# First attention: value product turned round (probabilities moving, values standing), result folded back by a product, and three of four second halves made on Pool

## The chip, the cores and the metric

One core of a Trainium2 chip runs the whole program. The time is the device time of one launch in microseconds: a median of 1862.45 over three runs (1860.44 to 1863.14). The engines of the core work in parallel, each through its own queue in order, and wait for one another on semaphores: TensorE (PE), VectorE (DVE), ScalarE (ACT), GpSimd (Pool), and SyncE (SP), which here issues most DMAs.

## What is computed

Two layers over x (2 x 512 tokens, 512 wide), each an attention over a context (2 x 1024 rows) and a feed-forward part; the second layer has 8-bit quantised keys, values, probabilities and ternary weights. The change is in the first layer's attention alone. It is plain causal attention with 16 heads of 32, the queries being the normalised x, and keys and values being the context itself:

```
qh, kh, vh = heads of q, k, v
scores = einsum('bhqd,bhkd->bhqk', qh, kh) / sqrt(32)
causal = ki <= qi + (Sk - Sq)            # Sq 512, Sk 1024
attn = softmax(where(causal, scores, -10000))
out = einsum('bhqk,bhkd->bhqd', attn, vh)
```

What follows depends on it exactly enough that a router's choice must not flip, so the kernel keeps fp32 accuracy by splitting: keys, queries and values are each three bf16 parts that sum to the fp32 value, and the probabilities are two fp16 halves, p1 (the rounded value) and p2 (the rest).

## The kernel before

The stages follow each other: context and key/value projection for the second layer (to about 175 us), layer norm and splitting (to 213), the first attention (213 to 572), router and expert feed-forward (to about 1190), then the second layer.

The first attention has 32 units, one for each batch and head (`UNITS`), which `sweep` runs on each engine: two written out, fifteen turns of a loop of two, the rest written out. In a unit the 512 queries meet 1024 keys in 8 key tiles of 128 (`KT`); because of the mask tiles 4 to 7 need only 512, 384, 256 and 128 queries (`WID`), 3328 columns in all. They are handled in four groups of two tiles: 1024, 1024, 896 and 384 columns. What is done per unit, with the lines:

- PE turns keys (L709) and queries (L717, L719) with transposes, so that the head's parts lie on partitions. These go through one PSUM bank, bank6. ACT copies the keys out of it to kA (`copy_keys`, L1137), DVE copies the first 64 rows again to kC (L1410) and copies the queries (L1414, L1415).
- For the softmax's maximum PE makes rough scores of the *next* unit, query tile by query tile, in two halves of `scores` (`smax`, L732 to L735); DVE takes the maxima (`take_max`, L1420) and splits them in two bf16 parts (`split_m`, L1427, L1429); PE turns these (`turn_m`, L741) and ACT copies them to two rows of qC (`copy_m`, L1141), where the exact score product takes the maximum off by itself.
- Exact scores, transposed (keys on partitions), are made tile by tile in bank4 and bank5 (`st`, L756 to L759). ACT turns each into exp in fp32 (eP, L1150), and a group into p1 (fp16, L1155). DVE makes p2 = eP - p1 (`rest_of_p`, L1434).
- `pv` (L773): for each key tile and each query tile of 128 that the mask leaves, p1 and p2 stand in the array (128x128, fp16) and 97 columns of values move through it (three parts of 32 and a column of ones, whose result is the softmax's sum). These are 26 pairs, 52 products of 97 columns per unit; they collect in bank7 with queries on partitions.
- `finish_unit` on DVE: the three parts are summed (L1440), the sum's reciprocal taken (L1442) and the product written to oatt (L1444).

The order is written out by hand in each engine's `att_unit`. PE's: the next unit's maxima tiles 0 and 1, scores 2 and 3, maxima tile 2, scores 4 and 5, pv 0 and 1, maxima tile 3, scores 6 and 7, turn the keys of the unit after the next, pv 2 and 3, turn the maxima, turn the queries, scores 0 and 1 of the next unit, pv 4 to 7. The first product of those scores 0 and 1 needs the maxima's rows from ACT; its start (L756) serves below as the unit's mark, the "restart". ACT's: for each group two exp and p1, at the end the keys' copy and the maxima's copy. DVE's: finish the unit before, then maxima, subtractions and copies in turn. SP loads three pieces per unit (`stage_unit`, L442, L443, L446). Pool has no work between 215.6 us and the scatter at 615 us (L568).

Of the kernel before, what the change touches and what calls it, by code (L numbers as in the profile page):

```python
# [25 lines left out]
F32 = mybir.dt.float32  # L26
# [29 lines left out]
KROW = KBLK * HD + 2  # L56
QROW = QBLK * HD
K3 = 3 * HD
K2 = 2 * HD
# [5 lines left out]
CONSTS = 13  # L65
# [53 lines left out]
def program(nc, x, ctx_in, gate_w, w1, w2, w3, Wq, bq, Wkv, bkv, Wp, bp, w_gate, w_up, w_down, ln_w, out):  # L119
    with ExitStack() as stack:  # L120
# [11 lines left out]
        class Region:  # L132
# [28 lines left out]
        xres = keep.take(F32, NT, D)  # L161
        vint = keep.take(BF16, NC, D)
# [6 lines left out]
        ones = keep.take(BF16, P)  # L169
        iota_e = keep.take(F32, E)  # L170
# [26 lines left out]
        v_step, vmax_ready, v_stored, v_back, v_made = (  # L197
            sem(n) for n in ("v_step", "vmax_ready", "v_stored", "v_back", "v_made"))
# [36 lines left out]
        p2 = ra.take(F16, NP)  # L235
        mx = ra.take(F32, QT)
        mparts = ra.take(BF16, QT, 2)
        osum = ra.take(F32, QT, HD)
# [110 lines left out]
        st_done, exp_done, p1_done, p2_done = (sem(n) for n in ("st_done", "exp_done", "p1_done", "p2_done"))  # L349
        pv_done, oread_done, o_done = (sem(n) for n in ("pv_done", "oread_done", "o_done"))  # L350
# [3 lines left out]
        zero_made = sem("zero_made")  # L354
# [30 lines left out]
        wpiece_done, wsum_done, wsum_all, w_mean = (sem(n) for n in ("wpiece_done", "wsum_done", "wsum_all", "w_mean"))  # L385
# [16 lines left out]
        def _(sp):  # L402
# [26 lines left out]
            sp.wait_ge(zero_made, 1)  # L429
# [84 lines left out]
        def _(pool):  # L514
# [22 lines left out]
            made(pool.iota(iota_s, pattern=[[1, SLOTS + 1]], base=0, channel_multiplier=0, allow_small_or_imprecise_dtypes=True))  # L537
            assert n == CONSTS
            pool.memset(zero, 0.0).then_inc(zero_made, 1)
            pool.memset(kvrow[:, :, :, :, KBLK * HD:KROW].rearrange("p b h t c -> p (b h t) c"), 1.0).then_inc(ones_set, 1)  # L540

# [9 lines left out]
            pool.partition_all_reduce(svrow, vam, P, bass.bass_isa.ReduceOp.absmax).then_inc(vmax_ready, 1)  # L551
            pool.wait_ge(vmax_ready, 1)

            pool.wait_ge(wsum_done, 1)
            pool.partition_all_reduce(wst[:, 1], wst[:, 0], P, bass.bass_isa.ReduceOp.add).then_inc(wsum_all, 1)
            pool.wait_ge(wsum_all, 1)
# [3 lines left out]
            for a in range(2):  # L560
                pool.memset(kC[a][K2:K2 + 2, :], 1.0).then_inc(ones_set, 1)

# [89 lines left out]
        def _(pe):  # L652
# [109 lines left out]
            def pv(u, a, k, r, first):  # L762
                if k == 0:
                    pe.wait_ge(v_in[a], 16 * (r + 1))
                    if not first:
                        pe.wait_ge(oread_done, 2 * u)
                if k % 2 == 0:
                    pe.wait_ge(p2_done, 4 * u + k // 2 + 1)
                    pe.wait_ge(p1_done, 4 * u + k // 2 + 1)
                for t in range(max(0, k - HALF), QT):  # L770
                    c = OFF[k] + (t * P - (SQ - WID[k]))
                    for part in (p1, p2):
                        ins = pe.matmul(bank7[:, t * 97:t * 97 + 97], part[:, c:c + P], vst[a][:, k, HD:HD + 97],  # L773
                                        start=(k == 0 and t == 0 and part is p1), stop=(k == KT - 1 and t == QT - 1 and part is p2),
                                        skip_group_check=True)
                if k % 2:
                    ins.then_inc(pv_done, 1)

            def att_unit(u, a, r, first, last):
# [3 lines left out]
                st(u, a, 2, first); st(u, a, 3, first)  # L783
                if not last:
                    smax(u + 1, b, 2)
                st(u, a, 4, first); st(u, a, 5, first)
                pv(u, a, 0, r, first); pv(u, a, 1, r, first)
                if not last:
                    smax(u + 1, b, 3)
                st(u, a, 6, first); st(u, a, 7, first)  # L790
# [9 lines left out]
                pv(u, a, 4, r, first); pv(u, a, 5, r, first)  # L800
                pv(u, a, 6, r, first); pv(u, a, 7, r, first)
# [17 lines left out]
            pe.wait_ge(oread_done, 2 * UNITS)  # L819
# [244 lines left out]
        def _(act):  # L1064
# [60 lines left out]
            act.wait_ge(vmax_ready, 1)  # L1125
# [9 lines left out]
            def copy_keys(u, b):  # L1135
                act.wait_ge(k0_turned, at(u))
                act.activation(kA[b], bank6[:].bitcast(BF16), ACT.Copy).then_inc(ka_ready, 1)  # L1137

            def copy_m(u, b):
                act.wait_ge(m_turned, at(u))  # L1140
                act.activation(qC[b][K2:K2 + 2, :], scores[:, 0:512].bitcast(BF16)[K2:K2 + 2, 0:SQ], ACT.Copy).then_inc(m_ready, 1)  # L1141

            def att_unit(u, a, k, first, last):
                b = 1 - a
                for g in range(4):
                    for j in (2 * g, 2 * g + 1):
                        if j == 2 * g and not first:
                            act.wait_ge(p2_done, 4 * (u - 1) + g + 1)
# [7 lines left out]
                if within(u + 2, UNITS):  # L1156
                    copy_keys(u + 2, a)
                if not last:
                    copy_m(u + 1, b)

            act.preload_act_table(ACT.Exp)
            copy_keys(0, 0)
            copy_m(0, 0)
            copy_keys(1, 1)
# [112 lines left out]
        def _(dve):  # L1277
# [59 lines left out]
            dve.wait_ge(wsum_all, 1)  # L1337
# [69 lines left out]
            def copy_keys(u, b):  # L1407

                dve.wait_ge(ka_ready, at(u))
# [21 lines left out]
            def rest_of_p(u, g):  # L1431
                s, e = OFF[2 * g], OFF[2 * g + 1] + WID[2 * g + 1]
                dve.wait_ge(p1_done, 4 * u + g + 1)
                dve.tensor_tensor(p2[:, s:e], eP[:, s:e], p1[:, s:e], ALU.subtract).then_inc(p2_done, 1)  # L1434

            def finish_unit(u, first):
# [324 lines left out]
```

## Time and profile before

| | |
|---|---|
| median of 3 runs | 1862.45 us |
| span of the profiled execution | 1858.6 us |
| PE / DVE / ACT / Pool busy over the span | 80 / 62 / 50 / 20% |
| first attention | 213 to 572 us |
| in 243 to 565 us: PE / DVE / ACT / Pool busy | 264 / 291 / 259 / 0 of 322 us |

The page gives for the profiled execution its span, from the first to the last instruction; its time as a run isn't listed apart, and the median of the runs is 3.85 us above the span. Busy times of one engine overlap a little from instruction to instruction, so an engine can be full below 100%: ACT's pair of exp takes 1.08 us though each lasts 0.59. Matmul durations contain a constant part that the next matmul hides; their pace is read from start to start.

### The profile page before, as it was taken

The page shows a single profiled execution, that of the slowest core. Times are in us where ns is not written, and L with a number is a line of the kernel's source. Part 1 is how long each engine was busy: PE and PEld are TensorE (multiplying, and loading weights), DVE is VectorE, ACT ScalarE, POOL GpSimd, SP SyncE. Part 2 cuts the span into 40 slices and gives each one's busy share as a digit, 9 for nine tenths or more (in the row PEclk, how much of TensorE's full clock was granted, in tenths as well). Part 3 has the DMA queues.
Part 4 walks back from the last instruction along what each step waited for, and adds up shares of the span by engine and source line. Part 5 has one row for each costly group of instructions (what it writes and reads, how often), then busy time and mean ns, then how long its engine had stood idle before and what let it go on. Part 6 is the DMA issues. An engine that isn't in the chain of part 4 may idle for free.

```text
span 1858.6 us, 30566 instructions
## 1 busy us (share of the span) xinstructions
PE 1482.2 (80%) x11006; PEld 830.7 (45%) x11064; DVE 1148.1 (62%) x2005; ACT 933.8 (50%) x1195; POOL 370.5 (20%) x179
## 2 busy tenths in 40 slices
PE   6885288888885299999999999277878787778777
PEld 3443155555554144444444444134545454444434
DVE  5888699899895211111111111569999999995565
ACT  3554388788783011111111111138998999892853
POOL 1101000000000366899940000320000000000150
PEclk9998599999997599999999999688999999999998
DMA  5567111121110699999988882640000000000101
GB/s 180 176 183 251 69 61 60 60 75 60 60 66 1 256 403 366 382 384 403 404 331 302 305 308 112 211 114 26 28 26 25 13 25 25 25 1 1 68 1 46
DMA packets 102757, 273.90 MB, mean 147 GB/s; under 512 B 7209, under 2 KB 11305, under 8 KB 101681
## 3 DMA queue, kind: packets, MB, share of 16 engines
q1 hardware_dynamic: 87904, 223.65, 32.4%
q0 software_dynamic: 10816, 40.90, 7.1%
q10 hardware_dynamic: 3984, 8.65, 1.2%
q8 instruction: 33, 0.54, 0.1%
q14 instruction: 20, 0.16, 0.0%
HBM read 212.62 MB, written 38.27 MB: 135 GB/s over the span
## 4 chain that ended last, share of the span: by engine, by line
PE 44%; DVE 34%; issue 11%; DMA 4%; ACT 3%; POOL 2%; SPq 1%; DVEq 1%; POOLq 0%; ACTq 0%
PE scores L859 17%; DVE arena L1615 15%; PE bank L875 9%; DVE arena L1420 6%; DVE arena L1434 3%; DMA arena<-in_ctx 2%; PE scores L686 2%; PE bank L773 2%; PE bank L1059 2%; PE bank L991 1%; PE bank L867 1%; DVE arena L1621 1%; PE bank L904 1%; PE bank L757 1%; PE scores L920 1%
## 5 line engine op out<-in xcount | busy, mean ns | idle before, releaser
L1615 DVE TENSOR_SCALAR_CACHE_REDUCE arena<-scores,arena 128x1024 f32<-128x1024 f32 x256 | 317.4, 1277 | 14.5 <-PE scores L920 14.3
L859 PE MATMUL scores<-arena 128*128 128x512 f32 x736 | 322.2, 596 | 0.8 <-DVE arena L1552 0.8
L1560 DVE TENSOR_TENSOR arena<-scores,arena 128x512 f32<-128x512 f32 x46 | 31.8, 692 | 447.7 <-PE scores L859 447.7
L1215 ACT ACTIVATE arena<-arena 128x2048 int16<-128x2048 f32 x128 | 256.3, 2002 | 47.9 <-DVE arena L1621 35.6
L920 PE MATMUL scores<-arena 96*128 96x512 bf16 x512 | 160.3, 400 | 88.9 <-DVE arena L1615 78.8
L859 PEld LDWEIGHTS scores<-arena 128*128 128x128 f32 x736 | 141.0, 192 | 178.0 <-issue 176.8
L875 PE MATMUL bank<-arena 128*128 128x512 f32 x368 | 163.3, 597 | 3.5 <-issue 3.3
L933 PEld LDWEIGHTS bank<-arena 128*128 128x128 bf16 x2048 | 122.8, 100 | 72.0 <-issue 68.3
L1183 ACT ACTIVATE arena<-scores 128x512 f32<-128x512 f32 x46 | 27.5, 597 | 249.1 <-PE scores L859 249.1
L933 PE MATMUL bank<-arena 128*128 128x128 bf16 x2048 | 141.5, 225 | 12.8 <-DVE arena L1640 1.7
L1150 ACT ACTIVATE arena<-bank 128x512 f32<-128x512 f32 (+3 forms) x256 | 117.8, 511 | 47.4 <-PE bank L757 36.4
L1434 DVE TENSOR_TENSOR arena<-arena 128x1024 f16<-128x1024 f32 (+2 forms) x128 | 129.9, 1016 | 1.6 <-ACT arena L1155 1.6
L1420 DVE TENSOR_REDUCE arena<-scores 128x1 f32<-128x640 f32 (+3 forms) x128 | 127.5, 1018 | 2.6 <-PE scores L735 2.6
L1224 ACT ACTIVATE arena<-bank 128x1024 bf16<-128x1024 int16 x128 | 128.3, 1002 | 1.2 <-PE bank L933 1.2
L1155 ACT ACTIVATE arena<-arena 128x1024 f16<-128x1024 f32 (+2 forms) x128 | 114.8, 897 | 11.5
L875 PEld LDWEIGHTS bank<-arena 128*128 128x128 f32 x368 | 68.2, 190 | 85.0 <-issue 85.0
L773 PE MATMUL bank<-arena 128*128 128x97 bf16 x1664 | 88.2, 207 | 19.8 <-DVE arena L1434 19.4
L920 PEld LDWEIGHTS scores<-arena 96*128 96x128 bf16 x512 | 31.6, 99 | 156.7 <-DVE arena L1615 144.2
L1189 ACT ACTIVATE arena<-bank 128x512 f32<-128x512 f32 x23 | 13.7, 597 | 166.8 <-PE bank L875 166.8
L568 POOL DMA_INDIRECT xs_d<-arena x16 | 15.6, 976 | 404.1 <-DVE arena L1541 399.5
L773 PEld LDWEIGHTS bank<-arena 128*128 128x128 f16 x1664 | 78.1, 97 | 36.9 <-issue 16.0
L757 PE MATMUL bank<-arena 66*128 66x512 bf16 (+3 forms) x256 | 86.3, 343 | 6.2 <-DVE arena L1410 6.1
(238 smaller groups left out, 2480.8 us busy)
## 6 DMA issues: line engine op xcount, KB each, us to landing
arena<-in_L_ffn_w SPq DMA_DIRECT2D x69, 2048.0 KB, 12.4
arena<-arena SPq DMA_DIRECT2D x64, 260.0 KB, 2.3
kst_d<-arena POOLq DMA_DIRECT2D x16, 384.0 KB, 6.4
tern_d<-arena POOLq DMA_DIRECT2D x12, 512.0 KB, 7.0
arena<-tern_d SPq DMA_DIRECT2D x3, 2048.0 KB, 10.8
arena<-kst_d SPq DMA_DIRECT2D x16, 384.0 KB, 3.5
xs_d<-arena SPq DMA_DIRECT2D x23, 256.0 KB, 3.6
arena<-xs_d SPq DMA_DIRECT2D x23, 256.0 KB, 13.2
```

The source lines that it names most:

```text
L773: ins = pe.matmul(bank7[:, t * 97:t * 97 + 97], part[:, c:c + P], vst[a][:, k, HD:HD + 97], start=(k == 0 and t == 0 and part is p1), stop ...
L859: ins = pe.matmul(scores[:, m * 1024 + half * 512:m * 1024 + half * 512 + 512], xsT[a][:, c], wa[:, m, c, half * 512:half * 512 + 512], st ...
L875: ins = pe.matmul(bank7[:, :], hT[:, c], wb[:, c], start=c == 0, stop=c == EC - 1)
L920: ins = pe.matmul(scores[:, s:s + 512], qhead[a][0:K3, t * P:(t + 1) * P], khead[a][0:K3, s:s + 512], start=True, stop=True)
L933: ins = pe.transpose(view[:, c * P:(c + 1) * P], p16[i][:, (8 * g + c) * P:(8 * g + c + 1) * P].bitcast(BF16), idb)
L1150: act.activation(eP[:, OFF[j]:OFF[j] + WID[j]], (bank4, bank5)[j % 2][:, 0:WID[j]], ACT.Exp, scale=SCALE).then_inc(exp_done, 1)
L1155: act.activation(p1[:, s:e], eP[:, s:e], ACT.Copy).then_inc(p1_done, 1)
L1215: act.activation(p16[i], ssb[i], ACT.Exp, bias=ebias[i], scale=-1.0, accum_out=rsum[a][:, t:t + 1]).then_inc(p_ready, 1)
L1224: act.activation(pT[t % 2][:, 8:16].rearrange("p c n -> p (c n)"), bank5[:].bitcast(I16), ACT.Copy).then_inc(pT_hi, 1)
L1420: dve.reduce_max(mx[:, t:t + 1], scores[:, s:s + 512 + (t + 1) * P], X).then_inc(max_done, 1)
L1434: dve.tensor_tensor(p2[:, s:e], eP[:, s:e], p1[:, s:e], ALU.subtract).then_inc(p2_done, 1)
L1615: dve.tensor_scalar(ssb[i][:, s:s + 1024], scores[:, s:s + 1024], nsq[:, bass.ds(h, 1), t], None, ALU.mult, ALU.min, accum_out=nmx[i][:, h ...
```

## The change

- The value product is turned round. The values of a key tile (128 x 97, bf16: `VR` = 97) stand, and p1 or p2 of all queries that the tile needs (fp16, `WID[k]` columns) moves: 16 products per unit. The result has the 97 value columns on partitions and the queries in the free dimension, in bank7.
- ACT copies that result to SBUF as fp32 (`copy_oT`, 97 x 512), after the first p1 of the next unit. PE then multiplies it with a constant `fold` (97 x 33, fp32: three identities under each other and a one for the sum), 4 products with the copied result standing (`fold_out`), which turns it back and adds the three parts. DVE's reduction goes; the reciprocal stays and the final product now reads PSUM.
- p2 of groups 0, 1 and 2 is made by Pool (`rest_of_p` in the gpsimd block), that of group 3 by DVE, as its last step in the unit.
- The keys' copy out of bank6 moves from ACT to DVE.
- PE's order: `fold_out` after scores 2 and 3, maxima tile 3 before pv 0 and 1. Pool makes four more constants at the start, on which PE's first wait counts; some semaphores are merged.

```diff
@@ Pool
+            made(pool.memset(fold, 0.0))
+            for j in range(3):
+                n_cols = OW if j == 2 else HD
+                made(pool.affine_select(out=fold[:, 0:n_cols], in_=fold[:, 0:n_cols], compare_op=ALU.not_equal, fill=1.0, base=-HD * j,
+                                        pattern=[[-1, n_cols]], channel_multiplier=1))
             assert n == CONSTS
...
+            def rest_of_p(u, a, k, first, last):
+                for g in range(3):
+                    s, e = OFF[2 * g], OFF[2 * g + 1] + WID[2 * g + 1]
+                    pool.wait_ge(p1_done, 4 * u + g + 1)
+                    pool.tensor_tensor(p2[:, s:e], eP[:, s:e], p1[:, s:e], ALU.subtract).then_inc(p2_done, 1)
+
+            sweep(pool, UNITS, rest_of_p)
@@ PE
             def pv(u, a, k, r, first):
                 if k == 0:
                     pe.wait_ge(v_in[a], 16 * (r + 1))
                     if not first:
-                        pe.wait_ge(oread_done, 2 * u)
+                        pe.wait_ge(o_step, 2 * u)
+                if k == KT - 2:
+                    pe.wait_ge(p2_last, at(u))
+                elif k % 2 == 0:
+                    pe.wait_ge(p2_done, 3 * u + k // 2 + 1)
                 if k % 2 == 0:
-                    pe.wait_ge(p2_done, 4 * u + k // 2 + 1)
                     pe.wait_ge(p1_done, 4 * u + k // 2 + 1)
-                for t in range(max(0, k - HALF), QT):
-                    c = OFF[k] + (t * P - (SQ - WID[k]))
-                    for part in (p1, p2):
-                        ins = pe.matmul(bank7[:, t * 97:t * 97 + 97], part[:, c:c + P], vst[a][:, k, HD:HD + 97],
-                                        start=(k == 0 and t == 0 and part is p1), stop=(k == KT - 1 and t == QT - 1 and part is p2),
-                                        skip_group_check=True)
+                w = WID[k]
+                for part in (p1, p2):
+                    ins = pe.matmul(bank7[0:VR, SQ - w:SQ], vst[a][:, k, HD:HD + VR], part[:, OFF[k]:OFF[k] + w],
+                                    start=k == 0 and part is p1, stop=k == KT - 1 and part is p2, skip_group_check=True)
                 if k % 2:
                     ins.then_inc(pv_done, 1)
...
+            def fold_out(u):
+                pe.wait_ge(oT_made, at(u))
+                for t in range(QT):
+                    ins = pe.matmul(bank7[:, t * OW:(t + 1) * OW], oT[0:VR, t * P:(t + 1) * P], fold[0:VR], start=True, stop=True)
+                ins.then_inc(o_folded, 1)
@@ ACT
+            def copy_oT(u, first):
+                act.wait_ge(pv_done, 4 * u + 4)
+                if not first:
+                    act.wait_ge(o_folded, at(u - 1))
+                act.activation(oT[0:VR], bank7[0:VR, :], ACT.Copy).then_inc(oT_made, 1)
...
                     act.activation(p1[:, s:e], eP[:, s:e], ACT.Copy).then_inc(p1_done, 1)
-                if within(u + 2, UNITS):
-                    copy_keys(u + 2, a)
+                    if g == 0 and not first:
+                        copy_oT(u - 1, not past(u, 2))
                 if not last:
                     copy_m(u + 1, b)
+                if last:
+                    copy_oT(u, False)
@@ DVE
             def copy_keys(u, b):
+                dve.wait_ge(k0_turned, at(u))
+                if past(u, 2):
+                    dve.wait_ge(st_done, KT * (u - 1))
+                dve.tensor_copy(kA[b], bank6[:].bitcast(BF16)).then_inc(ka_ready, 1)
                 dve.wait_ge(ka_ready, at(u))
                 dve.tensor_copy(kC[b][0:K2], kA[b][0:K2]).then_inc(kc_ready, 1)
...
             def att_unit(u, a, k, first, last):
                 b = 1 - a
-                if not first:
-                    finish_unit(u - 1, not past(u, 2))
                 if not last:
                     take_max(u + 1, 0)
                     take_max(u + 1, 1)
-                rest_of_p(u, 0)
+                if not first:
+                    finish_unit(u - 1)
                 if not last:
                     take_max(u + 1, 2)
-                rest_of_p(u, 1)
-                if not last:
                     take_max(u + 1, 3)
                     split_m(u + 1, False)
-                rest_of_p(u, 2)
                 if within(u + 2, UNITS):
                     copy_keys(u + 2, a)
-                rest_of_p(u, 3)
-                if within(u + 2, UNITS):
                     copy_q(u + 2, a)
+                rest_of_p(u)
```

## Rows read from the trace of the kernel before

**Rows 1.** The page's slices: busy tenths in 40 equal slices of the span.

```profile
DVE  5888699899895211111111111569999999995565
...
POOL 1101000000000366899940000320000000000150
```

**Rows 2.** Windows, steady attention: busy us and (instructions), then granted clock, DMA.

```profile
243.00:565.00 322.00, 263.62 (x3055) 177.59 (x3098) 291.03 (x477) 259.07 (x419) 0.00 (x0) 1.00 0.17 64
```

**Rows 3.** Waits, 243 to 565 us: who waited for whom, total, times, longest.

```profile
DVE arena L1440 <- PE bank L773: 24.4, 30, 1.6
...
PE bank L773 <- DVE arena L1434: 18.5, 30, 0.8
```

**Rows 4.** Lines by form, 243 to 565 us: busy us, mean ns, idle.

```profile
L773 PE MATMUL bank<-arena 128*128 128x97 bf16 x1560 | 82.7, 207 | 18.6 <-DVE arena L1434 18.5
L1150 ACT ACTIVATE arena<-bank 128x512 f32<-128x512 f32 x150 | 82.4, 591 | 33.0 <-PE bank L757 33.0
...
L1434 DVE TENSOR_TENSOR arena<-arena 128x1024 f16<-128x1024 f32 x60 | 73.0, 1216 | 0.0
...
L1434 DVE TENSOR_TENSOR arena<-arena 128x896 f16<-128x896 f32 x30 | 32.6, 1088 | 0.0
...
L1137 ACT ACTIVATE arena<-bank 128x1024 bf16<-128x1024 bf16 x29 | 29.1, 1005 | 0.0
...
L1440 DVE TENSOR_REDUCE arena<-bank 128x128 f32<-128x384 f32 x30 | 16.7, 558 | 24.4 <-PE bank L773 24.4
L1434 DVE TENSOR_TENSOR arena<-arena 128x384 f16<-128x384 f32 x30 | 16.3, 542 | 0.0
...
L1414 DVE COPY arena<-bank 128x512 bf16<-128x512 bf16 x29 | 11.8, 407 | 0.0
```

**Rows 5.** Timeline, first and last restart of 30 units: start us, us.

```profile
239.81 0.39 PE L756 MATMUL bank<-arena 128*128 128x512 bf16 x1
...
562.19 0.38 PE L756 MATMUL bank<-arena 128*128 128x512 bf16 x1 [0.72 <-issue]
```

**Rows 6.** Timeline, two units of the steady part.

```profile
287.20 1.22 DVE L1434 TENSOR_TENSOR arena<-arena 128x1024 f16<-128x1024 f32 x1
...
288.67 0.85 PE L773 MATMUL bank<-arena 128*128 128x97 bf16 x16 [0.71 <-DVE arena L1434]
...
302.90 0.39 PE L741 MATMUL scores<-arena 128*2 128x128 bf16 x4 [0.67 <-DVE arena L1429]
...
304.15 0.39 PE L756 MATMUL bank<-arena 128*128 128x512 bf16 x1 [0.20 <-ACT arena L1141]
...
304.80 1.08 ACT L1150 ACTIVATE arena<-bank 128x512 f32<-128x512 f32 x2 [0.88 <-PE bank L757]
...
305.97 1.06 ACT L1155 ACTIVATE arena<-arena 128x1024 f16<-128x1024 f32 x1
```

**Rows 7.** Pool's two-input operations by form, and one hand-over from ACT.

```profile
L616 POOL TENSOR_TENSOR arena<-arena 128x2048 bf16<-128x2048 bf16 x12 | 48.7, 4060 | 1.0
L648 POOL TENSOR_TENSOR arena<-arena 128x2048 f32<-128x2048 f32 x8 | 36.1, 4516 | 140.6 <-ACT arena L1263 140.6
...
1759.88 0.19 ACT L1263 ACTIVATION_READ_ACCUMULATOR arena<-arena 128x1 f32 x1
...
1760.15 4.52 POOL L648 TENSOR_TENSOR arena<-arena 128x2048 f32<-128x2048 f32 x1 [2.97 <-ACT arena L1263]
```

**Rows 8.** Window of the small fp32 products (L828); 96-column weight loads; a 1024-column copy.

```profile
594.00:597.69 3.69, 3.19 (x29) 3.22 (x29) 0.00 (x0) 1.64 (x2) 0.00 (x0) 0.98 0.00 0
...
108.10 0.91 PEld L663 LDWEIGHTS bank<-arena 128*96 128x96 bf16 x15 [0.30 <-issue]
...
L1640 DVE CAST arena<-bank 128x1024 bf16<-128x1024 int16 x128 | 87.6, 685 | 2.2 <-PE bank L933 2.2
```

**Rows 9.** Timeline, the stage's last product on DVE.

```profile
572.09 0.29 DVE L1444 TENSOR_TENSOR arena<-arena 128x128 f32<-128x128 f32 x1
```

**Rows 10.** Timeline, the second context tile's turn on PE.

```profile
13.30 1.12 PE L672 MATMUL bank<-arena 128*128 128x128 f32 x4 [6.82 <-DMA arena<-in_ctx]
```

More of the change, by code:

```diff
@@ L56 @@
 KROW = KBLK * HD + 2
+OW = HD + 1
 QROW = QBLK * HD
 K3 = 3 * HD
+VR = K3 + 1
 K2 = 2 * HD
@@ L169, in program @@
         ones = keep.take(BF16, P)
+        fold = keep.take(F32, OW)
         iota_e = keep.take(F32, E)
@@ L235, in program @@
         p2 = ra.take(F16, NP)
+        oT = Region(vint_at).take(F32, SQ)
         mx = ra.take(F32, QT)
         mparts = ra.take(BF16, QT, 2)
-        osum = ra.take(F32, QT, HD)
         rl = ra.take(F32, QT)
@@ L799, in att_unit @@
                     st(u + 1, b, 0, False); st(u + 1, b, 1, False)
-                pv(u, a, 4, r, first); pv(u, a, 5, r, first)
-                pv(u, a, 6, r, first); pv(u, a, 7, r, first)
+                for k in range(4, KT):
+                    pv(u, a, k, r, first)
+                if last:
+                    fold_out(u)
             turn_keys(0, 0, 0)
@@ L1146, in att_unit @@
                     for j in (2 * g, 2 * g + 1):
-                        if j == 2 * g and not first:
-                            act.wait_ge(p2_done, 4 * (u - 1) + g + 1)
+                        if j == KT - 2 and not first:
+                            act.wait_ge(p2_last, u)
+                        elif j % 2 == 0 and not first:
+                            act.wait_ge(p2_done, 3 * (u - 1) + g + 1)
                         act.wait_ge(st_done, KT * u + j + 1)
@@ L1429, in split_m, with rest_of_p, finish_unit @@
                 dve.scalar_tensor_tensor(mparts[:, :, 1], mx, -1.0, mparts[:, :, 0], ALU.mult, ALU.subtract).then_inc(m_step, 1)
[L1431 to L1436, printed above, removed]
-                dve.wait_ge(pv_done, 4 * u + 4)
-                if not first:
-                    dve.wait_ge(o_done, at(u - 1))
-                dve.tensor_reduce(osum, bank7[:, 0:4 * 97].rearrange("p (t c) -> p t c", t=QT)[:, :, 0:K3].rearrange("p t (c d) -> p t d c", d=HD),
-                                  X, ALU.add).then_inc(oread_done, 1)
-                dve.reciprocal(rl, bank7[:, 96:4 * 97:97]).then_inc(oread_done, 1)
-                dve.wait_ge(oread_done, 2 * u + 2)
+            def rest_of_p(u):
+                s = OFF[KT - 2]
+                dve.wait_ge(p1_done, 4 * u + 4)
+                dve.tensor_tensor(p2[:, s:NP], eP[:, s:NP], p1[:, s:NP], ALU.subtract).then_inc(p2_last, 1)
+            def finish_unit(u):
+                folded = bank7[:, 0:QT * OW].rearrange("p (t c) -> p t c", t=QT)
+                dve.wait_ge(o_folded, at(u))
+                dve.reciprocal(rl, bank7[:, HD:QT * OW:OW]).then_inc(o_step, 1)
+                dve.wait_ge(o_step, 2 * u + 1)
                 dve.tensor_tensor(oatt.rearrange("p b h t d -> p (b h) t d")[:, bass.ds(u, 1)].rearrange("p u t d -> p (u t) d"),
-                                  osum, each(rl, [QT, HD]), ALU.mult).then_inc(o_done, 1)
+                                  folded[:, :, 0:HD], each(rl, [QT, HD]), ALU.mult).then_inc(o_step, 1)
             def att_unit(u, a, k, first, last):
                 b = 1 - a
-                if not first:
-                    finish_unit(u - 1, not past(u, 2))
                 if not last:
```

48 lines of the change are left out of this document (23 added, 25 removed).

## Prediction

> **What bounds the kernel now.** The change touches the first attention only, so I went from the page's slices to that stretch: Pool shows zeros from the third slice to the tenth while VectorE (DVE) shows nines there [rows 1]. The view of windows puts numbers on the steady part, 243 to 565 us: in 322 us DVE is busy 291 (90%), PE 264, ScalarE (ACT) 259, Pool 0, at a granted clock of 1.00, the 2.4 GHz level [rows 2]. The view of waits says why DVE is not at 100%: 24.4 us in 30 waits for the last product with the values (L773), about 0.8 us per unit, and PE in its turn waits 18.5 us for DVE's subtraction (L1434) [rows 3]. DVE's own work and that one hand-over make the unit. The timeline has one fixed point per unit, the first score product of the next unit (L756, I call it the restart); it comes at 239.81 and, 30 units later, at 562.19 [rows 5]: 10.75 us per unit.
>
> **What goes from DVE, and what comes.** Per unit DVE loses the subtractions of 1024, 1024 and 896 columns (1.216 + 1.216 + 1.088) and the reduction of 0.558, 4.08 us; it gains the copy of the keys, which ACT did in 1.005 [rows 4] and which on DVE has as nearest row a 1024-column conversion out of PSUM at 0.685 [rows 8]. DVE's busy time falls from 291/30 = 9.7 to about 6.4 us per unit and no longer bounds. ACT loses 1.005 and gains the 97x512 copy of the result; nearest is its 512-column pass out of PSUM, 0.591 [rows 4]: 0.4 less, though this copy stands at a bad place, between the first p1 and the third exp. Bounds for these two copies are 0.41 (DVE's half as wide copy) to 1.0 and 0.5 to 1.0; I take the rows of equal width.
>
> **What comes on PE.** Sixteen products with 128 rows of p standing took 0.85 us with a last duration of 0.207 [rows 4, 6], so (0.85 - 0.21)/15 = 43 ns per 97 columns, 0.42 ns a column and 2.5 ns a product. Before: 52 x 43 ns = 2.24 us. After: 2 x 3328 = 6656 columns in 16 products, 2.81 us. The fold-back adds four fp32 products of 33 columns; the nearest are fp32 products with 8 columns, 29 in 3.19 us = 0.11 us each at a granted clock of 0.98 [rows 8], so 0.45 us, and up to 0.8 if they cost what half clock would make of them. PE rises by 1.0 us to about 9.1 us of issue, still under the period that follows.
> A weight load that isn't 128 columns wide is the one thing no attention row shows; of the nearest, 96 columns of bf16, fifteen went in 0.91 us, the last one's full duration included, so at most 61 ns apart [rows 8]; a 128-column product takes 56 at the pace above. I add nothing. The Trainium skill (TensorE: Matmul & The Clock Gate, Weight-path perf modes) says otherwise: the fast load needs exactly 128 weights, and without it a load takes columns/1.2, by estimate 81 ns for 97. By that rule the two 128-column products per unit (k = 7) would each stretch by some 25 ns, 1.5 us in all; the rows contradict it.
>
> **What comes on Pool.** Three subtractions per unit. Pool's two-input operations with 2048 columns take 4.516 us (fp32) and 4.060 (all bf16) [rows 7]. Ours has fp32 and fp16 in, fp16 out: between them, halved: 2.03 to 2.26, plus what is fixed in a Pool instruction. I take 2.25 for 1024 columns, 1.98 for 896: 6.5 us per unit, so Pool isn't full. The hand-over from ACT is short: a result ended at 1760.07 and Pool began at 1760.15 [rows 7], 0.1 us. From DVE's subtraction to PE's first product it was 287.20 + 1.22 = 288.42 to 288.67 [rows 6], 0.25 us; I use that for Pool to PE.
>
> **The new unit, walked from the restart (0).** In the rows the restart is at 304.15, the first exp at 304.80, its pair takes 1.08, the first p1 begins at 305.97 and takes 1.06 [rows 6].
> - ACT: exp pair 0.65 to 1.73, p1 group 0 1.82 to 2.88, copy of the result 2.78 to 3.37 (successive ACT passes overlap by 0.1: 2 x 0.591 - 1.08). PE needs 0.89 for the two restart tiles, 1.09 for the previous unit's last four value steps (2560 columns), 0.72 for two maxima tiles, 0.87 for two score tiles: the third exp can start at 3.35, the pair's second (its tile comes at 3.74) ends at 4.43.
> - p1 group 1: 4.53 to 5.59. Pool is free since 5.2 and subtracts from 5.67 to 7.92.
> - PE has everything before that step issued by 7.65 (16640 columns, the fold, and the walk's waits), so it waits 0.5 us and starts value steps 2 and 3 at 8.17; they take 4 x 0.217 = 0.87.
> - Then the old tail: the turn of the maxima starts at 302.90, ACT copies them, and the restart is at 304.15, 1.25 us in all [rows 6]. 8.17 + 0.87 + 1.25 = **10.29 us** per unit.
> DVE's queue fits in: maxima 0 and 1, reciprocal and product by 4.9, maxima 2 and 3 by 7.3, the split by 7.8 (needed at 9.04), keys by 9.0, queries by 10.7, and the last subtraction by 11.2, needed by PE at 10.29 + 1.64 + 0.25: nothing late. Its last subtraction is queued behind the wait for the turned queries; cover 0.5 us. So DVE's 3.4 us of relief become 10.75 - 10.29 = 0.46 us; what is late next is Pool's second subtraction, twice as long as DVE's and in the chain exp, p1, p2, value step, maxima turn, copy, restart. 30 x 0.46 = -13.8 us.
>
> **Outside the 30 units.** The last one has no next unit to cover Pool. Before, from the restart at 562.19 to the final product's end at 572.38 [rows 5, 9]: 10.19 us. After: p1 group 1 ends at 5.5 and group 2 (7/8 as wide) at 7.4; Pool's subtractions end at 7.84 and 9.90; value steps to 11.4, ACT's copy to 12.05, fold 0.25 + 0.6 to 12.9, reciprocal and product (0.17, 0.29, hand-over) to 13.6: +3.4 us. Ahead of the loop: the keys copy moved to DVE saves 0.3 us twice, and unit 0 waits for Pool 0.3 longer: -0.3. Four more constants on Pool lie before PE's first wait, at about 0.3 each; the second context tile is what PE waits for until 13.30 [rows 10], so they cost nothing; without that cover, 1 us. DMAs: the unit's three loads and their waits are as they were, and kst is issued once the v load has gone, at about 2.2 in the new unit, 5 us ahead of need.
>
> **Sum.** -13.8 + 3.4 - 0.3 = -10.7 us. The profiled execution's span, 1858.6, would become 1847.9; the median 1862.45 lies 3.85 above that span, so the time is **1851.8 us**.
>
> **Rivals.**
> - *Pool quicker than its rows* (1.75 us or less; for it, nothing but that the rows are of other types). Then PE's own queue is the bound, value steps 2 and 3 start at 7.65: 9.77 us per unit, 30 x -0.98 = -29.4, +3 - 0.3: 1836 us. Chance 0.08.
> - *Pool slower beside DVE* (the slower side). Pool now shares every unit with a DVE in full work, while its rows of 4.51 to 4.53 us stood beside operations out of PSUM. Place: the first two subtractions, back to back once each exceeds 2.7 us. With x for one, the value steps start at 2.96 + 2x + 0.3. The unit is at its old 10.75 from x = 2.7, and at x = 3.0 it is 9.26 + 2.12 = 11.4 us: 30 x 0.63 + 4.5 = +23, 1886 us. Against it: DVE's remaining two-SBUF-input work is one subtraction of 0.54 us [rows 4], which falls where Pool has slack. Chance 0.14. The Trainium skill (GPSIMD Engine Reference, Key points) names that sharing: the SBUF interfaces are contended with DVE instructions that have two SBUF inputs or run in a two-port mode. No row of this trace has the pair.
> - *The relief doesn't arrive*: Pool at 2.5, a Pool hand-over of 0.4 and a fold of 0.8 give 10.29 + 0.25 + 0.15 + 0 (the fold has 0.5 us of cover) = 10.69, and with +3.8 for the end the time is 1864. Chance 0.14.
> - *My walk*: 0.64, with Pool between 2.05 (10.09 per unit, 1845.6) and 2.4 (10.44, 1856.5).
>
> **Numbers.** A difference under 0.2% (3.7 us) can't be told from none. Faster by more: the walk and the quick Pool, 0.72; within: most of the third rival and the walk's edge, 0.12; slower: the slow Pool and a remainder, 0.16. The range 1838 to 1864 holds the walk and the third rival and leaves out both Pool extremes.
>
> **What would show it.** A restart every 10.3 us; Pool's 1024-column subtraction at 2.25 us; PE waiting half a microsecond for Pool before value step 2, and for ACT's copy of the maxima before the restart; DVE at 62% in the stage; the value products 0.217 us apart; the end from last restart to last product 13.6 us; the rest of the kernel shifted and otherwise equal. It is wrong if Pool's subtraction differs by over 0.3 us, if 97-column weights slow the products, or if PE never waits for Pool.

## The result, and the profile after

| kernel | median of its runs, us | lowest to highest | ratio to before, 95% interval |
|---|---|---|---|
| before | 1862.78 (12 runs) | 1860.27 to 1873.60 | |
| after | 1875.61 (12 runs) | 1871.55 to 1885.79 | 1.0068 [1.0048, 1.0088] |
| forecast | 1851.8 | 1838 to 1864 | |

The change makes the kernel 0.7% slower where 0.6% faster was forecast. One execution of a later kernel (the fold done twice, below) took 2406.62 us at a granted clock of 0.64, far off its seven others; its median has it in, its ratio hasn't. The profiled execution of after has a span of 1875.1 us and took 1876.78. I divided both spans by marks in the trace: DVE's memset that ends the layer norm stage, the first and the last start of ACT's copy of the maxima (one per unit, 30 units between them) and the last product written to oatt.

| us | before | after | difference | forecast |
|---|---|---|---|---|
| ahead of the first attention | 213.6 | 217.3 | +3.7 | 0 |
| to the first copy of maxima | 25.45 | 25.70 | +0.25 | -0.3 |
| 30 units | 322.48 | 331.23 | +8.75 | -13.8 |
| per unit | 10.75 | 11.04 | +0.29 | -0.46 |
| from the last copy to the end of the attention | 10.87 | 14.32 | +3.5 | +3.4 |
| the rest | 1286.2 | 1286.5 | +0.3 | 0 |

The differences sum to +16.5, the forecast to -10.7; 22.5 of the 27.2 us between them lie in the 30 units. The 3.7 us at the top come where both kernels run the same code but for four constants (below, unexpected).

First the page of after: the slices in tenths, then the costliest group of Pool. Pool now works from the sixth slice to the thirteenth, and DVE, which had eights and nines from the sixth to the twelfth [rows 1], shows sevens.

```profile
DVE  5888677777776211111111111568999999995565
...
POOL 1011055555552356899950000320000000000150
PEclk9998599999997599999999999598999999999998
...
L576 POOL TENSOR_TENSOR arena<-arena 128x1024 f16<-128x1024 f32 (+1 forms) x96 | 195.1, 2047 | 170.1 <-ACT arena L1189 170.1
```

The view of windows of after, 243 to 565 us, beside [rows 2]:

```profile
243.00:565.00 322.00, 289.28 (x2187) 186.45 (x2218) 250.11 (x382) 240.66 (x408) 176.86 (x87) 1.00 0.17 63
```

DVE falls from 291 to 250 us, PE rises from 264 to 289, the granted clock stays at 1.00, and yet fewer units fit in. The view of waits of after (250 to 550 us; total, times, longest; three dots stand for lines left out, here and below) names what ended the idle time:

```profile
POOL arena L576 <- ACT arena L1189: 134.1, 55, 4.4
...
ACT arena L1167 <- PE scores L758: 38.3, 27, 1.4
...
PEld scores L758 <- DVE arena L1467: 32.1, 27, 1.2
...
PE scores L758 <- DVE arena L1467: 19.5, 27, 0.8
PEld bank L734 <- DVE arena L1446: 10.5, 26, 0.4
...
PE bank L734 <- DVE arena L1446: 5.9, 27, 0.3
```

The forecast expected PE to wait for Pool (L576). In these 300 us it never does: PE waits for L1467, the second step of splitting the maxima, an operation of four columns. The groups of the window 243 to 565 us by form (busy total, mean ns):

```profile
L576 POOL TENSOR_TENSOR arena<-arena 128x1024 f16<-128x1024 f32 x58 | 123.5, 2130 | 143.4 <-ACT arena L1189 143.4
...
L576 POOL TENSOR_TENSOR arena<-arena 128x896 f16<-128x896 f32 x29 | 54.6, 1882 | 0.0
...
L1467 DVE SCALAR_TENSOR_TENSOR arena<-arena 128x4 bf16<-128x4 f32 x29 | 51.8, 1785 | 1.0
...
L802 PEld LDWEIGHTS bank<-arena 97*128 97x128 f32 x232 | 29.6, 191 | 5.2 <-ACT arena L1173 3.3
L802 PE MATMUL bank<-arena 97*128 97x33 f32 x232 | 28.3, 266 | 0.0
...
L1446 DVE COPY arena<-bank 128x1024 bf16<-128x1024 bf16 x30 | 20.3, 678 | 0.0
```

In before the same instruction was L1429 and took 0.166 us on average. It now takes 1.785, with the same four columns. The timeline of one unit (start, duration, in brackets the idle time before it) shows what it lies beside:

```profile
271.57 3.97 POOL L576 TENSOR_TENSOR arena<-arena 128x1024 f16<-128x1024 f32 x2 [0.54 <-ACT arena L1189]
...
273.57 0.17 DVE L1465 TENSOR_SCALAR arena<-arena 128x4 bf16<-128x4 f32 x1
273.78 1.78 DVE L1467 SCALAR_TENSOR_TENSOR arena<-arena 128x4 bf16<-128x4 f32 x1
...
273.87 1.03 PE L793 MATMUL bank<-arena 128*97 128x512 f16 x4
...
275.62 0.38 PE L758 MATMUL scores<-arena 128*2 128x128 bf16 x4 [0.72 <-DVE arena L1467]
276.04 0.59 ACT L1167 ACTIVATE arena<-scores 2x512 bf16<-2x512 bf16 x1 [1.42 <-PE scores L758]
```

Pool's second and third subtraction follow each other, change over near 273.66 and end at 275.54. DVE's operation, started at 273.78, ends at 275.56. The first step of the split (L1465), begun in the last tenth of a microsecond of Pool's second subtraction, took its usual 0.17. PE could have begun the turn of the maxima at 273.87 + 4 x 0.217 = 274.74 and began at 275.62: 0.88 us later. The turn leads through ACT's copy to the next unit's restart, so the unit pays for all of it.

### The profile page after: what moved, and what is told of

Its sections match the earlier page's. It is cut to its first block, busy times and chain, and to the rows that moved or that the text cites. A ratio compares the mean times of both kernels' runs of the same rounds, so it can differ in the third digit from the quotient of the medians.

```text
span 1875.1 us, 28953 instructions
## 1 busy us (share of the span) xinstructions
PE 1523.0 (81%) x10125; PEld 846.5 (45%) x10168; DVE 1109.7 (59%) x1909; ACT 921.1 (49%) x1195; POOL 565.9 (30%) x279
## 4 chain that ended last, share of the span: by engine, by line
PE 53%; DVE 26%; issue 10%; DMA 3%; ACT 3%; POOL 2%; SPq 1%; DVEq 1%; POOLq 0%; ACTq 0%
PE scores L889 17%; DVE arena L1646 15%; PE bank L905 9%; PE bank L793 3%; PE bank L774 3%; PE bank L773 2%; DMA arena<-in_ctx 2%; PE scores L749 2%; PE scores L703 2%; PE bank L1089 2%; PE bank L1021 1%; PE bank L802 1%; DVE arena L1652 1%; PE bank L897 1%; DVE arena L1446 1%
## 5 line engine op out<-in xcount | busy, mean ns | idle before, releaser
L576 POOL TENSOR_TENSOR arena<-arena 128x1024 f16<-128x1024 f32 (+1 forms) x96 | 195.1, 2047 | 170.1 <-ACT arena L1189 170.1
L655 POOL COPY arena<-arena 128x512 bf16 (+1 forms) x16 | 9.8, 614 | 375.5 <-PE bank L976 375.5
L793 PE MATMUL bank<-arena 128*97 128x512 f16 (+3 forms) x512 | 105.9, 339 | 2.2 <-POOL arena L576 1.9
L1671 DVE CAST arena<-bank 128x1024 bf16<-128x1024 int16 x128 | 88.0, 688 | 2.2 <-PE bank L963 2.2
```

Of the source, the lines that this page charges most:

```text
L576: pool.tensor_tensor(p2[:, s:e], eP[:, s:e], p1[:, s:e], ALU.subtract).then_inc(p2_done, 1)
L793: ins = pe.matmul(bank7[0:VR, SQ - w:SQ], vst[a][:, k, HD:HD + VR], part[:, OFF[k]:OFF[k] + w], start=k == 0 and part is p1, stop=k == KT ...
```

## The experiments

The theory after these rows: a DVE operation that reads SBUF in a certain way is held until the Pool instruction under way ends, and this costs 0.88 us per unit. Rivals: the new value product or the fold on PE is the cost; or DVE's work was never worth moving.

**One input instead of two.** Split_m's second step left out the low half of the maximum:

```diff
-dve.scalar_tensor_tensor(mparts[:, :, 1], mx, -1.0, mparts[:, :, 0], ALU.mult, ALU.subtract)
+dve.tensor_scalar(mparts[:, :, 1], mx, 0.0, None, ALU.mult)
```

> The changed kernel, but the second half of the maxima (L1467) is made by a tensor_scalar with one input (the maximum times 0) in place of a scalar_tensor_tensor with two; the low half of the maximum is left out. Theory (a DVE operation with two SBUF inputs waits until the Pool subtraction that runs beside it has ended): the operation takes 0.2 us instead of 1.78, the turn of the maxima follows value step 3 at once, the unit falls from 11.03 to 7.93 + 0.87 + 1.25 = 10.05 us and the time to 1875.6 - 30 x 0.98 = 1846. Rival 1 (TensorE is the bound with its 0.9 us fold, and the long DVE operation only fills a gap): no change, 1875. Rival 2 (any DVE operation out of SBUF is held, with one input too): the operation still takes 1.8 us, 1875.

1876.07 us, ratio 1.0068 [1.0041, 1.0096]: no change from after. The row of its L1467 (min/median/max ns):

```profile
L1467 DVE TENSOR_SCALAR arena<-arena x32: 172/1792/1807, 227.1 to 570.2; 128x4 bf16<-128x4 f32 x32
```

The operation with one SBUF input is held as long as that with two (median 1.792 against 1.784 us). "Only two inputs" fell; the hold itself did not. Whether the hold costs the time, or PE would be no sooner without it (Rival 1), this run can't say.

**All subtractions back on DVE**, everything else as after:

```diff
-            sweep(pool, UNITS, rest_of_p)
+            def first_rests(u, g):        # on DVE
+                dve.wait_ge(p1_done, 4 * u + g + 1)
+                dve.tensor_tensor(p2[:, s:e], eP[:, s:e], p1[:, s:e], ALU.subtract).then_inc(p2_done, 1)
```

> The changed kernel with all four subtractions on DVE again (Pool idle in the stage), the rest of the change kept. Theory: the operation L1467 is back at 0.17 us, and DVE is the bound as before the change: 9.7 - 0.56 + 0.69 = 9.8 us busy per unit and a hand-over of up to 0.9, 10.4 to 10.8 us per unit, 1858 to 1868. Rival 1 (TensorE's added work is what makes the unit 11.0): 11.0 per unit, 1875. Rival 2 says as the theory.

1954.26 us, 1.0494 [1.0463, 1.0525], 13.84 us per unit: neither the theory (10.4 to 10.8) nor Rival 1 (11.0) came. Later the same with the keys' copy ahead of the third subtraction:

```diff
                 if within(u + 2, UNITS):
                     copy_keys(u + 2, a)
+                first_rests(u, 2)
```

> The version with all subtractions on DVE (1954), the copies of the keys moved ahead of the third subtraction. Theory (there the keys' copy was late behind 1.08 us of subtraction, TensorE stood still for 1.2 us and its clock fell to the 1.2 GHz level in part of each unit): the gap goes, the clock stays at 2.4 GHz, the unit falls from 13.8 to 10.5 to 10.9 us, 1855 to 1867. Rival (DVE is simply too full, and the clock follows from that): 13 us or more, over 1930.

1906.95 us, 1.0226 [1.0185, 1.0266], 11.97 us per unit. The windows of 243 to 565 us, the first kernel and then the second (PE, PEld, DVE, ACT, Pool busy, granted clock):

```profile
243.00:565.00 322.00, 277.12 (x1779) 165.59 (x1777) 236.90 (x374) 199.23 (x330) 0.00 (x0) 0.89 0.14 52
```

```profile
243.00:565.00 322.00, 287.79 (x2047) 169.38 (x2046) 272.54 (x430) 224.11 (x379) 0.00 (x0) 1.00 0.15 57
```

In both the second step of the split is back at 0.166 us, so the hold needs Pool. But in the first the keys' copy stood behind a subtraction of 1.08 us, PE waited 1.2 us for it in each unit, and the granted clock fell to 0.89: in the unit around 250 us PE was busy 5% of 251 to 252 us, and the clock was at 0.50, the 1.2 GHz level, from 254 to 256 us. The second restores 1.00 and 1.87 us per unit by one moved line. Its 11.97 us met neither expectation. No engine is full there, and I can't name one wait that makes it; it stays open. In both orders tried the change without Pool is worse than with it (1906.95 at best, against 1875.61).

**The third subtraction behind the split.** Pool's last one waits until the split is done:

```diff
                     pool.wait_ge(p1_done, 4 * u + g + 1)
+                    if g == 2 and not last:
+                        pool.wait_ge(m_step, 2 * u + 4)
```

> The changed kernel, but Pool's third subtraction waits until DVE has split the maxima of the next unit; nothing is left out. Theory: L1467 runs between two Pool operations and takes 0.2 us; the third subtraction begins some 0.4 us later, which has cover until value step 4; 10.05 to 10.2 us per unit, 1846 to 1851. Rival 1: 1875. Rival 2 (held whatever it reads): as the theory here, since Pool is idle at that moment.

1844.62 us, 0.9899 [0.9872, 0.9926], 10.17 us per unit. The timeline of one unit:

```profile
277.29 0.17 DVE L1467 TENSOR_SCALAR arena<-arena 128x4 bf16<-128x4 f32 x1
277.50 0.17 DVE L1469 SCALAR_TENSOR_TENSOR arena<-arena 128x4 bf16<-128x4 f32 x1
...
277.74 1.89 POOL L578 TENSOR_TENSOR arena<-arena 128x896 f16<-128x896 f32 x1 [0.32 <-DVE arena L1469]
...
278.55 0.38 PE L760 MATMUL scores<-arena 128*2 128x128 bf16 x4
278.61 1.30 DVE L1450 COPY arena<-arena 64x1024 bf16<-64x1024 bf16 x1
```

One wait on Pool takes 0.87 us out of each unit (11.04 to 10.17) and turns a loss of 13 us into a gain of 18. Of these 31 us the 30 units make 26; in the profiled executions another 3.5 lie ahead of the attention (213.8 us against 217.3). Pool still has the same work beside the same DVE. What is held now is the second keys' copy, 1.30 us instead of 0.42: it starts at 278.61 and ends 0.28 us behind Pool's end (277.74 + 1.89 = 279.63). No wait for it stands in this run's view of waits.

**Two subtractions on Pool**, the third on DVE behind the keys' copy:

```diff
-                for g in range(3):            # Pool
+                for g in range(2):
...
+                rest_of_p(u, 2)               # DVE, behind copy_keys
```

> The changed kernel, but only groups 0 and 1 are subtracted on Pool; group 2 (896 columns) is on DVE, after the keys' copy. Theory: Pool's second subtraction has ended when DVE splits the maxima, L1467 takes 0.2 us; DVE gains 1.09 us and has room (6.4 of 10 us); 10.05 to 10.2 us per unit, and the last unit ends about 1 us earlier since DVE's subtraction is faster: 1845 to 1850. Rival 1: 1875.

1853.77 us, 0.9943 [0.9925, 0.9960], 10.22 us per unit: the same unit as in the experiment before, by another way. The total misses the expected 1845 to 1850. It is 9.2 us higher than in the experiment before, and so much lies ahead of the attention in its profiled execution (222.9 against 213.8 us).

**Single operations beside Pool.** No layer is computed here, and there is one execution: DVE runs twelve kinds of operation alone, beside a Pool subtraction of 2048 columns, and beside a one-input Pool operation of 2048 columns. A reduction out of PSUM stands between any two of them.

```diff
+for i in range(13): pool.tensor_tensor(pc, pa, pb, ALU.subtract)
+for i in range(13): pool.tensor_scalar(pd, pa, 2.0, None, ALU.mult)
+dve: each operation once alone, once in each of Pool's two rows
```

> None of the layers is computed; the output is a constant. Twelve DVE operations, each once alone, once started 0.3 us into a Pool tensor_tensor of 2048 columns (4 us), once into a Pool tensor_scalar of 2048 columns (5.4 us). Theory, widened after the one-input form was held as well (1.79 us): DVE operations with two SBUF inputs, and those with one SBUF input and no PSUM operand that DVE runs at more than one element per cycle (tensor_scalar, copies), are held until the Pool operation ends, 3 to 4 us longer than alone; those out of PSUM and the reduction (one element per cycle) are not. Rival: only small operations, or only the 4-column one, are held; then the 512-column ones take their time alone. Open: whether Pool's one-input operation holds them too.

The timeline (two lines of the part alone, then the first part beside Pool), and three operations (ns min/median/max over alone and the two companies):

```profile
5.95 1.80 POOL L59 MEMSET pd<- 128x2048 f32 x1
5.96 1.82 DVE L43 TENSOR_SCALAR q<-s 128x4 bf16<-128x4 f32 x1
...
18.13 28.91 POOL L64 TENSOR_TENSOR pc<-pa,pb 128x2048 f16<-128x2048 f32 x7 [10.38 <-DVE m L88]
22.29 0.42 DVE L95 TENSOR_REDUCE m<-ps 128x1 f32<-128x256 f32 x1 [4.32 <-POOL pc L64]
22.75 3.58 DVE L42 SCALAR_TENSOR_TENSOR o<-s,t 128x4 bf16<-128x4 f32 x1
26.42 0.42 DVE L95 TENSOR_REDUCE m<-ps 128x1 f32<-128x256 f32 x1
26.88 3.60 DVE L43 TENSOR_SCALAR q<-s 128x4 bf16<-128x4 f32 x1
```

```profile
L45 DVE COPY ho<-ha x3: 293/3721/5030, 8.9 to 94.6; 128x512 bf16<-128x512 bf16 x3
...
L49 DVE TENSOR_TENSOR fo<-ps,fb x3: 691/691/692, 12.7 to 116.5; 128x512 f32<-128x512 f32 x3
L50 DVE TENSOR_REDUCE r<-fa x3: 685/686/686, 13.9 to 122.0; 128x1 f32<-128x512 f32 x3
```

| operation of DVE | alone | beside Pool, two inputs | beside Pool, one input |
|---|---|---|---|
| two SBUF inputs, 4 columns | 0.16 | 3.58 | 3.14 |
| one input, 4 columns, fp32 to fp32 | 0.17 | 3.60 | 4.91 |
| one input, 4 columns, fp32 to bf16 | 1.82 (beside a memset of Pool) | 3.60 | 4.91 |
| one input, 512 columns, fp32 | 0.43 | 3.70 | 5.00 |
| copy, 512 columns, bf16 / fp32 | 0.29 / 0.43 | 3.72 / 3.77 | 5.03 / 5.09 |
| copy of every second column, bf16 | 0.43 | 3.85 | 5.16 |
| two SBUF inputs, 512 columns | 0.69 | 3.97 | 3.54 |
| PSUM and SBUF input, 512 columns | 0.69 | 0.69 | 0.69 |
| copy out of PSUM, 512 columns | 0.69 | 0.69 | 0.69 |
| reduction in SBUF, 512 columns | 0.69 | 0.69 | 0.69 |
| reciprocal, 4 columns | 0.18 | 0.18 | 0.18 |

Pool's subtraction takes 4.05 us, the first one alone as well as those beside a held operation, so the hold costs Pool nothing. The longest took 4.39: it began at 51.31 us, while DVE's held two-input operation of 512 columns was itself at work until 51.78, so Pool can be held up by DVE as well. A held operation costs what remains of the Pool instruction (3.3 to 3.4 us here, since the reduction ahead took 0.42) plus itself, whether it has 4 columns or 512. Four kinds are never held. The last column shows that one-input Pool operations hold too, and one row that was to run alone shows it for a memset: it fell beside Pool's and ended 0.03 us after it.

**Before plus Pool alone.** The kernel before, its product untouched, with three subtractions on Pool:

```diff
+            def rest_of_p(u, a, k, first, last):   # Pool, as in after
+            sweep(pool, UNITS, rest_of_p)
...
-                rest_of_p(u, 0)                    # DVE; also (u, 1) and (u, 2)
```

> The kernel before the change, with the subtractions of groups 0, 1 and 2 moved to Pool and nothing else (values moving, reduction on DVE, keys' copy on ACT). Theory (the hold is a matter of Pool beside DVE, not of the new value product): the split L1429 or L1427 is held as in the changed kernel, up to 1.8 us, and the unit stays near 10.7 to 11.2 us: 1860 to 1876. Rival (the turned-round product and the fold are what lengthened the unit): DVE is relieved of 3.5 us and TensorE has no added work, 9.7 to 10.0 us per unit, 1830 to 1840.

1876.42 us, 1.0063 [1.0037, 1.0089], 10.90 us per unit. Its timeline:

```profile
269.12 1.88 POOL L568 TENSOR_TENSOR arena<-arena 128x896 f16<-128x896 f32 x1
269.49 1.54 DVE L1440 TENSOR_SCALAR arena<-arena 128x4 bf16<-128x4 f32 x1
271.07 0.17 DVE L1442 SCALAR_TENSOR_TENSOR arena<-arena 128x4 bf16<-128x4 f32 x1
```

The loss is there without the new product. Its size is best read in the units, since 9.2 us of this profiled execution lie ahead of the attention (222.8 us against 213.6): 10.90 us, 0.15 more than before although DVE has three subtractions less to do. The hold takes the first step of the split here, as that one comes upon Pool's third subtraction under way.

**The last unit's subtractions on DVE**, with the ordered Pool:

```diff
-            sweep(pool, UNITS, rest_of_p)
+            sweep(pool, UNITS - 1, rest_of_p)
+                if last:                      # DVE
+                    for g in range(3): ...
```

> The version with Pool's third subtraction behind the split of the maxima (median 1844.6), and the last unit's subtractions all on DVE, which has nothing else to do there. Pool took 1.88 and 2.13 us where DVE takes 1.09 and 1.22, and 0.9 us of DVE's last one was the hold: the end shortens by 1.5 to 2.5 us, to 1842 to 1843. If the end is bound by ACT and TensorE instead: unchanged, 1844.6.

1848.68 us, 0.9921 [0.9890, 0.9952], against 1844.62 for the ordered kernel: a miss, 1842 to 1843 was expected. In the trace the end of the attention shortens from 14.4 to 13.3 us, 1.1 of the 3.5 us that it had grown; in the total it can't be seen.

**The old product, ordered.** The kernel before plus Pool plus the wait; then also with the keys' copy on DVE:

```diff
+                    if g == 2 and not last:
+                        pool.wait_ge(m_step, 2 * u + 4)
...
-                    copy_keys(u + 2, a)       # ACT; second kernel alone
+                dve.tensor_copy(kA[b], bank6[:].bitcast(BF16)).then_inc(ka_ready, 1)
```

> The kernel before the change with the three subtractions on Pool, the third behind the split of the maxima; the old value product (values moving), reduction on DVE, keys' copy on ACT. Theory (the hold was all that cost; the turned-round product takes 1.5 us of TensorE per unit and gives DVE back only 0.56 - 0.69 us, so it isn't needed): no hold, value steps 2 and 3 at 7.8 us after the restart, ACT's keys' copy and maxima's copy end at 9.7, 9.8 to 10.0 us per unit, 1835 to 1841. Rival (the gain of the ordered version comes from the new product as well): 10.4 us or more, over 1850.

> The same with the keys' copy out of PSUM on DVE, as in the changed kernel. Theory: ACT loses 1.0 us ahead of the maxima's copy, the chain exp, p1, Pool, value steps, turn, copy is left: 7.8 + 0.7 + 1.25 = 9.75 us or somewhat less per unit, 1830 to 1836. Rival (DVE or the chain through Pool bounds e6 already): as e6.

1848.20 us, 0.9919 [0.9890, 0.9948], 10.04 us per unit, a miss of the expected total (its profiled execution took 1842.09) and just of the expected unit; and 1838.34 us, 0.9865 [0.9834, 0.9896], 9.84 per unit, span 1832.9, which leaves the expected range by 2. The window 243 to 555 us of the second:

```profile
243.00:555.00 312.00, 270.66 (x3127) 181.71 (x3170) 260.30 (x438) 236.57 (x401) 190.56 (x93) 0.99 0.18 66
```

The first kernel shows the wait's worth once more: 10.90 to 10.04 us per unit. The second is the fastest kernel of all, 24 us under before, and has nothing of the new product. Beside the ordered kernel with the new product (10.17 us, PE busy 303.54 of the same 312 us) it shows that once the hold is gone the turned product, with its fold, its copy on ACT and the orders of PE and DVE that came with it, costs 0.33 us per unit; how that divides among them wasn't tested.

**The fold done twice**, in the ordered kernel and in after:

```diff
-                for t in range(QT):
+                for t in range(2 * QT):
+                    t = t % QT
```

> The ordered version of the changed kernel (median 1844.6), the four fold products made twice; 0.8 us more of TensorE per unit, result unchanged. Theory (with the hold gone TensorE is the bound, busy 305 of 322 us): the unit grows from 10.17 by 0.7 to 0.8 us, to 1866 to 1870. Rival (Pool's second subtraction bounds the unit): under 0.3 us more per unit, under 1855.

> The changed kernel (median 1875.6) with the four fold products made twice. Theory (its unit is set by the end of Pool's third subtraction, which follows from ACT's p1 and not from the fold): value steps 2 and 3 end 0.8 us later, at the moment at which the held operation ends: 0 to 0.3 us more per unit, 1876 to 1885. Rival (TensorE is the bound of the changed kernel): 0.8 us more per unit, 1900.

1880.07 us, 1.0076 [1.0047, 1.0105], 11.05 per unit (+0.89); and 1910.85 us, 1.0245 [1.0211, 1.0278], 12.11 per unit (+1.07). The first is in kind what PE as the bound says, but above the expected 1866 to 1870; the second keys' copy, held by Pool as before, is now waited for in most units:

```profile
PE bank L776 <- DVE arena L1451: 10.8, 26, 0.5
```

So its 0.89 us isn't the fold alone. The second kernel missed what my theory said by 26 us and contradicts its step that the fold has cover. Its timeline:

```profile
270.69 1.87 PE L803 MATMUL bank<-arena 97*128 97x33 f32 x16
...
272.39 0.38 PE L749 MATMUL scores<-arena 128*128 128x512 bf16 x1
...
275.62 1.88 POOL L576 TENSOR_TENSOR arena<-arena 128x896 f16<-128x896 f32 x1 [0.72 <-ACT arena L1190]
275.65 1.87 DVE L1466 TENSOR_SCALAR arena<-arena 128x4 bf16<-128x4 f32 x1
...
277.78 0.38 PE L758 MATMUL scores<-arena 128*2 128x128 bf16 x4 [0.80 <-DVE arena L1468]
```

Two folds hold PE from 270.69 to 272.39, 0.85 each. All that follows on PE is later by one fold: its score tile, ACT's passes, Pool's third subtraction. The hold ends with that subtraction and moves along. The remaining 0.2 us fit the second step of the split: it now stands behind the held first one (L1466), where in after it was the held one itself. So the hold doesn't absorb a delay of PE; the two add up.

## Why the prediction was wrong

- **The failed step is the one on what is queued beside Pool.** In "Pool slower beside DVE" I argued that "DVE's remaining two-SBUF-input work is one subtraction of 0.54 us". It had another in the split, L1429, for which PE waited 0.67 us before the turn of the maxima already [rows 6], and so in every unit, by a line of the view of waits of before (243 to 565 us) that I passed over:

```profile
PE scores L741 <- DVE arena L1429: 18.2, 30, 0.7
```

And I looked for the cost on the wrong engine: Pool wasn't slowed, DVE was held. The walk had "the split by 7.8 (needed at 9.04)"; held until Pool's end it cost 0.88 us per unit. Ordering Pool behind it gave 0.87 back, and the same hold without the new product cost the kernel before its gain. 10.29 + 0.88 would be 11.17, measured 11.04. This cause is shown. The prediction's own sign of being wrong, that PE never waits for Pool, came true in the steady part. DVE was busy 78% there (250 of 322 us) where 62% was forecast; 52 us of it are the held operation.

- **What a page would have given.** The row is 1.785 us, ending 0.02 us after Pool. The Trainium skill (SBUF — State Buffer, SBUF: two separate sides) says that DVE and Pool share one pair of ports as an exclusive lock, held for a whole instruction, where the other engine blocks fully; the DVE operations concerned run in a 2-port mode or have two SBUF inputs. The hold until Pool's end agrees, and nothing with an input out of PSUM was ever held; the earlier release beside Pool's one-input operation (below, unexpected) doesn't fit a lock held to the end. I had taken only the sentence on sharing, and as a slowdown.
- **The rival on the slower side** gave 1886 at x = 3.0 for the stretch of Pool's operations. Sign and pair of engines were right, the mechanism wasn't: Pool's operations took 2.130 and 1.882 us, quicker than the 2.25 and 1.98 taken from other types. The 0.14 for it was too little, since no row of before had the pair at all.
- **The fold** was put at 0.45 us, at most 0.8, with 0.5 of cover. Each of its four fp32 products stands as two records (232 in 29 units, 8 per unit), and the fold takes 0.81 us on PE (280.65 to 281.46 in one unit of after). The cover was used up: the forecast half microsecond of PE's waiting for Pool before value step 2 didn't come [rows 3 had DVE's subtraction there]; the page gives 1.9 us of such waits in all 32 units, none of them between 250 and 550 us. The quicker Pool and the longer fold cancelled in the period, which the ordered kernel shows: 10.17 us where 10.29 was walked, by a PE that is busy 304 of 312 us. The walk's number was near by luck: PE was the bound, not the chain through Pool.
- **The 97-column loads** cost nothing that the products show: eight value products with 2560 columns took 1.25 us, less the last one's 0.22 leaves 1.03 for 2432 columns, 0.42 ns each, the pace without any gap. The load itself is longer, 125 ns on average against 97 for 128 columns. The Trainium skill (TensorE: Matmul & The Clock Gate, Weight-path perf modes) expects that direction. The 81 ns that the prediction estimated for it were too few, and the stretch of the 128-column products didn't come: the moving columns cover the load.
- **Right within 0.3 us**: the end of the attention (+3.5 for +3.4), ACT's copy of the result (0.579 for 0.591), the keys' copy (0.678 for 0.685), the constants at no cost (213.8 us ahead of the attention in the ordered kernel, 213.6 in before), the place of value step 2 (7.93 after the restart for 8.17, though PE's own queue set it and not Pool). The start of the attention was 0.5 off, the rest of the kernel 0.3.
- **A misreading without effect**: the prediction has Pool at zero from the third slice to the tenth and DVE at nines there. By the page [rows 1] Pool has a one in the fourth slice and zeros from the fifth to the thirteenth, and DVE has eights and nines from the sixth to the twelfth.

## What to carry to other kernels

Before work goes to Pool, list every DVE operation that will run beside it and ask of each whether it may be held until Pool's instruction ends: short ones on a hand-over to PE first, since four columns waited as long as 512. If one is on the path, order Pool's instruction behind it with one wait, or give that work another place: here that one wait was worth 0.87 us in each of 30 units. And test the parts of a change alone: the turned product, which was to relieve DVE of a reduction, cost 0.33 us per unit with what came with it, and without it the rest was the fastest kernel.

## What the runs showed of the hardware, unexpected

- One-input DVE operations on SBUF are held by Pool too, even with 4 columns and with every second column read (0.17 to 3.60, 0.43 to 3.85 us). Reductions, reciprocals and whatever reads PSUM are not.
- Against a one-input Pool operation of 5.36 us, DVE's operations with two SBUF inputs came out earlier (3.14 and 3.54 us) than those with one (4.91 to 5.16), and over a microsecond before Pool's end. I have no tested reason.
- The time ahead of the attention differs from kernel to kernel by up to 14 us with the same code but for the constants: 213.6, 213.8, 215.1, 217.3, 222.9 and 227.6 us in six of them, one profiled execution each. With it goes the granted clock of the first 185 us (0.96 in before, 0.94 in after, 0.91 in the slowest of these). How much of the spread of the medians it makes isn't shown, since only one execution of each has a trace; the units' period leaves it out and so was the better measure. Its cause stays open.
